# Attention in a decoder layer: the context products of two units issued together, behind the second score of every even unit

## The chip, the cores and the metric

One core of one Trainium2 chip. The metric is the device time of one execution of the whole program in microseconds; lower is better. The kernel before has a median of 1931.85 us over three runs (1931.19 to 1934.34).

## What is computed

A decoder layer on x of 8 sequences x 512 tokens x 512, in float32: a Mamba-2 block, a cross-attention and a soft mixture of experts, each added to its input and normalized. The change touches the cross-attention:

```python
q = (x @ Wq.T + bq).reshape(B, N, HEADS, HEAD_DIM).transpose(0, 2, 1, 3)
k = (context @ Wk.T + bk).reshape(B, M, HEADS, HEAD_DIM).transpose(0, 2, 1, 3)
v = (context @ Wv.T + bv).reshape(B, M, HEADS, HEAD_DIM).transpose(0, 2, 1, 3)
attn = jax.nn.softmax(jnp.einsum('bhnd,bhmd->bhnm', q, k) * scale, axis=-1)
out = jnp.einsum('bhnm,bhmd->bhnd', attn, v)
out = out.transpose(0, 2, 1, 3).reshape(B, N, C)
return out @ Wo.T + bo
```

B is 8, N = M = 512, 16 heads of 32 columns.

## The kernel before

The program runs three stages one after the other: `mamba_stage`, `attention_stage`, `moe_stage`. Inside a stage, each engine runs its own list of instructions, and semaphores tie them together. TensorE is called PE in the profile, ScalarE ACT, VectorE DVE, GpSimd POOL, SyncE SP (it issues most of the DMAs).

The attention takes one sequence per turn. The 16 heads lie in four groups (`gr`) of four heads (`AG`), and the 512 context rows in four tiles (`u`), so a turn has 16 units n = 4 gr + u. In the names of steps below, the three numbers are group, tile and head. The scores are computed twice, since the softmax needs the maximum of each query's row before the exponentials of the transposed scores:

- "p1" (L2156, PE): scores of one head with the queries on the partitions, into one of five *shared* PSUM banks. DVE takes the extreme of each row (L2026, "the maximum"), and ACT takes the exp with the row's sum (L1963, "sum"), in place; after that the bank is free.
- "split" and "neg": the four heads' maxima of a group are split in two, transposed by PE (L2162), copied by ACT (L1970) and written by DMA into two more rows of the stacked queries.
- "st" (L2174, PE): the transposed scores of one head and one context tile, with the maxima taken off, into one of two *scores* banks. ACT takes the exp (L1956) into `probs`, a buffer with two places, one per unit, used in turn.
- "av" (L2185, PE): the context product of one unit. Its four heads are four matmuls of 32 columns each, next to each other in the array; each is recorded twice, so a unit has eight records. The four tiles of a group add up in the bank `o_bank`.
- "recip", "inv", "norm", "osplit": DVE inverts the sums, POOL spreads them (L1910), PE transposes them (L2192), DVE copies them out (L2042) and multiplies `o_bank` with them (L2046), then splits the result (L2051, L2054).
- "qk", "v" (L2128) and "out" (L2202): the projections of q, k and v for the next turns and the output projection, each in two halves of six matmuls, also in shared banks. A q or k projection is copied by ACT (L1948) and then read by DVE (L2013); v is copied by DVE (L2020); an output tile is read by DVE (L2068). The bank is free after DVE's part.
- "xt", "c": transposes and splits of the next input.

One list sets the order of all this, for all engines: `attention_order`. For each unit it goes through four heads. At each head it puts the maxima that are due (`MAXIMA`, 64 per turn, some 22 heads ahead of the scores), the score, the sums that are to be done by now (`totals(left)` leaves that many for later, by `LAGS`), and half a projection where `HALF_AT` says so. After the fourth head of unit n it puts the product of unit n - 1. An engine that has no part in a step skips it. Two waits tie the products to the rest. The exp of a unit's first head needs the product of two units before, since it overwrites its place in `probs`:

```python
if h == 0 and (n >= 2 or not t.first()):
    act.wait_ge(av_done, t.at(UNITS, n - 1))
```

and a score needs the exp of two scores before, for its bank:

```python
pe.wait_ge(exp_ready, t.at(AG * UNITS, AG * n + h + 1 - SCORE_BANKS))
```

`bank_plan` deals out the shared banks in the order of the steps, and `take` on PE waits for the last reader of the bank. So the place of a step in the list also decides whose reader it waits for. The lists are unrolled for the first turn, for three steady turns in a loop, and for the last turn and what remains of it (`parts_of`, `over_attention`).

## Time and profile before

| | us |
|---|---|
| median of the runs (lowest, highest) | 1931.85 (1931.19, 1934.34) |
| profiled execution: span from its first to its last instruction | 1924.5 |
| PE busy in the span | 1825.8 (95%) |
| DVE busy | 1433.6 (74%) |
| ACT busy | 1266.8 (66%) |
| POOL busy | 468.5 (24%) |

The profiled execution's own time is not given apart from its span; the median of the three runs is 7.35 us above the span. The context products run from 879.0 to 1646 us of the span, which is the attention's stretch. Seven turns (seven of the eight sequences) take 97.7 to 101.7 us each there, five of them 99.8; the last is shorter, since nothing is projected ahead in it. Times in a timeline are counted from the start of the span. A matmul record of 512 columns is about 0.40 us long, but the next one starts 0.23 us after it, since they are pipelined: the distance of two starts is what it costs. The same holds, less so, for ACT and DVE.

### The profile page before, as it was taken

The numbers are of one execution on the slowest core, as the hardware profiler recorded it, in microseconds if no ns is written. First come the engines' busy times: TensorE is split into PE (matmuls) and PEld (weight loads), VectorE is DVE, ScalarE is ACT, GpSimd is POOL, SyncE is SP. The second block draws the span as 40 slices with busy tenths as digits, with TensorE's granted clock in tenths as the row PEclk, the third lists the DMA queues.
The fourth block names the chain that finished last, engine by engine and source line by source line (L and its number), as shares of the span: only waits on it lengthen the run. The fifth ranks groups of instructions, "written<-read, shape, count | busy, mean of one in ns | idle before, by whom it ended". The sixth has DMA issues, their size and how long they took to land. (4 is left out here: it accounts for less than half of the span.)

```text
span 1924.5 us, 39071 instructions
## 1 busy us (share of the span) xinstructions
PE 1825.8 (95%) x12780; PEld 1308.2 (68%) x12780; DVE 1433.6 (74%) x2902; ACT 1266.8 (66%) x3128; POOL 468.5 (24%) x661
## 2 busy tenths in 40 slices
PE   7899999999999999778999999999999999899988
PEld 5677777777787878555666666666666664588853
DVE  7978888888888888646786767777776766666348
ACT  5646454555555555348988888888989888366614
POOL 1312121212121313331323232322222233100006
PEclk9999999999999999889999999999999999899999
DMA  7113131313131312333343333434343423821266
GB/s 236 53 49 103 46 105 46 106 45 107 40 111 38 114 35 94 137 102 97 89 111 111 111 111 100 122 89 116 87 123 90 129 67 102 259 95 50 75 209 257
DMA packets 120045, 200.61 MB, mean 104 GB/s; under 512 B 23088, under 2 KB 44592, under 8 KB 119600
## 3 DMA queue, kind: packets, MB, share of 16 engines
q1 hardware_dynamic: 110640, 179.20, 30.1%
q0 software_dynamic: 9216, 18.89, 4.0%
q8 instruction: 118, 1.93, 0.4%
q14 instruction: 71, 0.58, 0.1%
HBM read 117.27 MB, written 29.88 MB: 76 GB/s over the span
## 5 line engine op out<-in xcount | busy, mean ns | idle before, releaser
L2026 DVE TENSOR_REDUCE a_mx<-a_shared 128x1 f32<-128x512 f32 x512 | 329.5, 681 | 56.6 <-PE a_shared L2156 54.5
L1963 ACT ACTIVATE a_shared<-a_shared,a_mx 128x512 f32<-128x512 f32 x512 | 340.9, 668 | 22.7 <-DVE a_mx L2026 22.2
L1956 ACT ACTIVATE a_probs<-a_scores 128x512 f32<-128x512 f32 x512 | 300.5, 600 | 67.9 <-PE a_scores L2174 64.7
L2156 PE MATMUL a_shared<-a_ks,a_qs 96*128 96x512 f32 x512 | 208.2, 427 | 14.5 <-ACT a_shared L1963 10.4
L2174 PE MATMUL a_scores<-a_qs,a_ks 98*128 98x512 f32 x512 | 201.2, 404 | 5.6 <-ACT a_probs L1956 5.5
L2128 PE MATMUL a_shared<-link 128*128 128x512 f32 x768 | 199.1, 395 | 1.1 <-DVE a_qk_lo L2013 1.1
L1083 PE MATMUL m_proj<-m_xt_hi,link 128*128 128x512 f32 x448 | 182.4, 407 | 3.8 <-DVE m_acc L777 3.4
L597 ACT ACTIVATE m_xw<-m_added,m_wdt 128x64 f32<-128x64 f32 x256 | 56.0, 329 | 192.5 <-DVE m_xdt L865 192.5
L2156 PEld LDWEIGHTS a_shared<-a_ks,a_qs 96*128 96x128 f32 x512 | 94.1, 190 | 129.2 <-ACT a_shared L1963 57.6
L1084 PE MATMUL m_proj<-m_xt_lo,link 128*128 128x512 f32 x448 | 177.1, 395 | 0.0
L1085 PE MATMUL m_proj<-m_xt_hi,link 128*128 128x512 f32 x448 | 176.2, 393 | 0.0
L777 DVE SCALAR_TENSOR_TENSOR m_acc<-m_proj,m_cw,m_acc 128x511 f32<-128x511 f32 (+2 forms) x216 | 159.3, 747 | 17.6 <-ACT m_acc L536 12.4
L2128 PEld LDWEIGHTS a_shared<-link 128*128 128x128 f32 x768 | 144.6, 190 | 34.7 <-DVE a_qk_lo L2013 1.5
L2185 PE MATMUL a_o_bank<-a_probs,a_v 128*32 128x512 f32 x1024 | 137.7, 610 | 0.0
L491 POOL TENSOR_TENSOR m_ssum<-m_ssum,m_sq 128x512 f32<-128x512 f32 x56 | 72.4, 1293 | 262.3 <-ACT m_sq L607 167.3
L2174 PEld LDWEIGHTS a_scores<-a_qs,a_ks 98*128 98x128 f32 x512 | 97.3, 191 | 34.1 <-ACT a_probs L1956 16.3
L1790 POOL DMA_DIRECT2D a_ks<-a_k_hi x192 | 95.2, 503 | 80.3 <-DVE a_qk_lo L2013 42.1
L1963 ACT ACTIVATION_READ_ACCUMULATOR a_shared<-a_shared,a_mx 128x1 f32 x512 | 109.5, 214 | 0.0
L1083 PEld LDWEIGHTS m_proj<-m_xt_hi,link 128*128 128x128 f32 x448 | 84.7, 189 | 27.8 <-DVE m_acc L777 7.5
L1085 PEld LDWEIGHTS m_proj<-m_xt_hi,link 128*128 128x128 f32 x448 | 84.5, 189 | 20.1
L1084 PEld LDWEIGHTS m_proj<-m_xt_lo,link 128*128 128x128 f32 x448 | 84.6, 189 | 16.7
L880 DVE SCALAR_TENSOR_TENSOR m_st<-m_st,m_whole,m_added 128x64 f32<-128x64 f32 x384 | 90.8, 278 | 6.8
(306 smaller groups left out, 3925.3 us busy)
## 6 DMA issues: line engine op xcount, KB each, us to landing
m_dec<-step_decay SPq DMA_DIRECT2D x64, 256.0 KB, 4.0
a_qs<-link SPq DMA_DIRECT2D x256, 64.0 KB, 2.0
m_ce<-run_decay SPq DMA_DIRECT2D x128, 112.0 KB, 3.1
a_ks<-a_k_hi POOLq DMA_DIRECT2D x192, 64.0 KB, 2.5
e_x<-x SPq DMA_DIRECT2D x11, 1024.0 KB, 5.6
m_xt_in<-x_t_in SPq DMA_DIRECT2D x8, 1024.0 KB, 9.2
m_x_tok<-x_in SPq DMA_DIRECT2D x8, 1024.0 KB, 5.3
x<-m_x_tok SPq DMA_DIRECT2D x32, 256.0 KB, 2.7
```

The lines of the kernel that those rows point to most:

```text
L777: ins = dve.scalar_tensor_tensor(out=acc[:, slot, s:SEQ], in0=proj[tile % 2][:, 0:SEQ - s], scalar=cw[:, n, 2 - i:3 - i], in1=acc[:, slot, ...
L1083: pe.matmul(bank[:, :], wh, xt_hi[:, k, :], start=(k == 0), stop=False)
L1084: pe.matmul(bank[:, :], wh, xt_lo[:, k, :], start=False, stop=False)
L1085: ins = pe.matmul(bank[:, :], wl, xt_hi[:, k, :], start=False, stop=(k == KT - 1))
L1790: eng.dma_start(dst[:, h, :].bitcast(F32), part[h * AD:(h + 1) * AD, :].bitcast(F32)).then_inc(stack_in[queue][gr % 2], 16)
L1956: act.activation(probs[:, n % 2, h, :], scores[t.score_bank(n, h)][:, :], ACT.Exp, scale=-1.0).then_inc(exp_ready, 1)
L1963: act.activation(scored[:, :], scored[:, :], ACT.Exp, scale=-1.0, bias=mx[:, i % 2, j, h:h + 1], accum_out=den[:, i, j, h:h + 1]).then_inc ...
L2026: dve.tensor_reduce(mx[:, i % 2, j, h:h + 1], bank(what)[:, :], AX.X, ALU.min).then_inc(mx_ready, 1)
L2128: ins = pe.matmul(bank(what)[:, :], *pair, start=(k == n == 0), stop=(k == KT - 1 and n == 2))
L2156: pe.matmul(bank(what)[:, :], qs[0:STACK, t.slot(i), h, j * P:(j + 1) * P], ks[0:STACK, t.slot(i), h, :], start=True, stop=True).then_inc( ...
L2174: pe.matmul(scores[t.score_bank(n, h)][:, :], ks[0:STACK + 2, t.slot(i), h, j * P:(j + 1) * P], qs[0:STACK + 2, t.slot(i), h, :], start=Tr ...
L2185: ins = pe.matmul(o_bank[rows, :], v[:, j, i * P + hh * AD:i * P + (hh + 1) * AD], probs[:, n % 2, hh, :], start=(j == 0), stop=(j == TT - 1))
```

## The change

The product of each unit no longer follows the next unit's fourth score. In an even unit, right behind its second score (`PAIR_AT = 1`), two products are issued in a row: in a group's first unit (u = 0) those of the last two tiles of the group before, after the transposes of the inverse sums and followed by the normalization; in its third unit (u = 2) those of the first two tiles of this group. Before the first score of an even unit all pending sums are put (`totals(0)`), and after the second unit of a group up to two may be left.

```diff
-LAGS = (2, 1, 0, 0)
+LAGS = (2, 1, 2)
+PAIR_AT = 1
...
+        group, d = (gr - 1, 0) if n >= TT else (KT - 1, -1)
         for h in range(AG):
             for _ in range(-(-(h + 1) * MAXIMA[n] // AG) - -(-h * MAXIMA[n] // AG)):
                 maximum()
                 totals(LAGS[0])
+            if h == 0 and u % 2 == 0:
+                totals(0)
             put("st", gr, u, h, 0)
-            totals(LAGS[1] if h < AG - 1 else LAGS[2])
+            totals(LAGS[1] if h < AG - 1 else LAGS[2] * (n % TT == 1))
             ended()
+            if h == PAIR_AT and u == 0:
+                put("inv", group, 0, 0, d)
+                for j in (TT - 2, TT - 1):
+                    put("av", group, j, 0, d)
+                put("norm", group, 0, 0, d)
+            elif h == PAIR_AT and u == 2:
+                for j in (0, 1):
+                    put("av", gr, j, 0, 0)
             for half in range(2):
                 if HALF_AT[n][half] == h:
                     large(n, half)
         if u == TT - 1:
             put("recip", gr, 0, 0, 0)
-        group, d = (gr - 1, 0) if n >= TT else (KT - 1, -1)
-        if u == 0:
-            put("inv", group, 0, 0, d)
-        put("av", *((gr, u - 1, 0, 0) if u else (group, TT - 1, 0, d)))
-        totals(LAGS[3])
-        if u == 0:
-            put("norm", group, 0, 0, d)
```

Five lines are added above the attention's code, so L2185 of the kernel before is L2190 after, and so on.

On PE, the end of unit 11 and unit 12 of a steady turn before. The rows are: p1 and the last score of unit 11, the product of unit 10, p1 and the first score of unit 12, half a k projection, and so on:

```order
L2156 MATMUL a_shared2<-a_ks,a_qs 128x512
L2174 MATMUL a_scores1<-a_qs,a_ks 128x512
L2185 MATMUL a_o_bank<-a_probs,a_v 32x512 x4
L2117 REGISTER_ALU
L2156 MATMUL a_shared3<-a_ks,a_qs 128x512
L2174 MATMUL a_scores0<-a_qs,a_ks 128x512
L2128 MATMUL a_shared4<-link 128x512 x6
L2117 REGISTER_ALU
L2156 MATMUL a_shared0<-a_ks,a_qs 128x512
L2174 MATMUL a_scores1<-a_qs,a_ks 128x512
L2128 MATMUL a_shared4<-link 128x512 x6
```

The same place after the change:

```order
L2161 MATMUL a_shared2<-a_ks,a_qs 128x512
L2179 MATMUL a_scores1<-a_qs,a_ks 128x512
L2122 REGISTER_ALU
L2161 MATMUL a_shared3<-a_ks,a_qs 128x512
L2179 MATMUL a_scores0<-a_qs,a_ks 128x512
L2133 MATMUL a_shared4<-link 128x512 x6
L2122 REGISTER_ALU
L2161 MATMUL a_shared0<-a_ks,a_qs 128x512
L2179 MATMUL a_scores1<-a_qs,a_ks 128x512
L2197 MATMUL a_shared1<-a_ident,a_inv_rows 128x128 x4
L2190 MATMUL a_o_bank<-a_probs,a_v 32x512 x8
L2133 MATMUL a_shared4<-link 128x512 x6
```

The product of unit 10 has left its place ahead of unit 12, and comes with that of unit 11 behind the transposes, between the two halves of the k projection. The first half of that projection writes shared4 in both, the bank that the q projection just before it used.

On ACT, the change from unit 11 to unit 12 before: two sums, the exps of unit 12's first two heads, a sum, and the copy of the k projection:

```order
L1963 ACTIVATE a_shared0,a_den<-a_shared0,a_mx 128x512
L1959 REGISTER_ALU
L1963 ACTIVATE a_shared2,a_den<-a_shared2,a_mx 128x512
L1955 REGISTER_ALU
L1956 ACTIVATE a_probs<-a_scores0 128x512
L1956 ACTIVATE a_probs<-a_scores1 128x512
L1959 REGISTER_ALU
L1963 ACTIVATE a_shared3,a_den<-a_shared3,a_mx 128x512
L1768 REGISTER_ALU
L1948 ACTIVATE a_k_hi<-a_shared4,bcol 128x512
```

And after:

```order
L1968 ACTIVATE a_shared0,a_den<-a_shared0,a_mx 128x512
L1964 REGISTER_ALU
L1968 ACTIVATE a_shared2,a_den<-a_shared2,a_mx 128x512
L1964 REGISTER_ALU
L1968 ACTIVATE a_shared3,a_den<-a_shared3,a_mx 128x512
L1960 REGISTER_ALU
L1961 ACTIVATE a_probs<-a_scores0 128x512
L1961 ACTIVATE a_probs<-a_scores1 128x512
L1773 REGISTER_ALU
L1953 ACTIVATE a_k_hi<-a_shared4,bcol 128x512
```

The third sum has moved ahead of the two exps, and nothing stands between them and the copy of the projection.

## Rows read from the trace of the kernel before

**Rows 1.** Windows of one steady turn: busy time (and instructions) of each engine, granted clock, DMA.
```profile
core 0: us, PE busy (x) PEld busy (x) DVE busy (x) ACT busy (x) POOL busy (x), PEclk, DMA share, GB/s
1045.90:1145.70 99.80, 99.03 (x499) 66.38 (x496) 73.85 (x137) 87.98 (x213) 27.86 (x46) 1.00 0.38 107
```

**Rows 2.** Timeline of PE, units 11 and 12: start us, us, instruction.
```profile
1137.70 0.40 PE L2128 MATMUL a_shared<-a_xt_hi,link 128*128 128x512 f32 x1
...
1139.08 0.39 PE L2156 MATMUL a_shared<-a_ks,a_qs 96*128 96x512 f32 x1
1139.31 0.39 PE L2174 MATMUL a_scores<-a_qs,a_ks 98*128 98x512 f32 x1
1139.63 1.07 PE L2185 MATMUL a_o_bank<-a_probs,a_v 128*32 128x512 f32 x8
1140.63 0.50 PE L2156 MATMUL a_shared<-a_ks,a_qs 96*128 96x512 f32 x1
1140.96 0.40 PE L2174 MATMUL a_scores<-a_qs,a_ks 98*128 98x512 f32 x1
1141.20 1.53 PE L2128 MATMUL a_shared<-link 128*128 128x512 f32 x6
1142.57 0.39 PE L2156 MATMUL a_shared<-a_ks,a_qs 96*128 96x512 f32 x1
```

**Rows 3.** Timeline of PE, windows 1113.40:1113.74 and 1113.40:1113.76: records begun.
```profile
1113.30 0.64 PE L2185 MATMUL a_o_bank<-a_probs,a_v 128*32 128x512 f32 x4
...
1113.30 1.04 PE L2185 MATMUL a_o_bank<-a_probs,a_v 128*32 128x512 f32 x5
```

**Rows 4.** Timeline of ACT, units 11 and 12; in brackets the idle time before.
```profile
1139.36 0.69 ACT L1948 ACTIVATE link<-a_shared,bcol 128x512 fp32r<-128x512 f32 x1
...
1143.23 0.60 ACT L1956 ACTIVATE a_probs<-a_scores 128x512 f32<-128x512 f32 x1 [0.50 <-PE a_scores L2174]
1143.73 0.66 ACT L1963 ACTIVATE a_shared<-a_shared,a_mx 128x512 f32<-128x512 f32 x1
...
1144.69 0.69 ACT L1948 ACTIVATE a_k_hi<-a_shared,bcol 128x512 fp32r<-128x512 f32 x1 [0.19 <-PE a_shared L2128]
1145.28 0.59 ACT L1956 ACTIVATE a_probs<-a_scores 128x512 f32<-128x512 f32 x1
1145.76 0.66 ACT L1963 ACTIVATE a_shared<-a_shared,a_mx 128x512 f32<-128x512 f32 x1
```

**Rows 5.** Timeline of DVE, units 11 and 12.
```profile
1140.08 0.75 DVE L2013 SCALAR_TENSOR_TENSOR a_qk_lo<-a_shared,bcol,link 128x512 fp32r<-128x512 f32 x1 [1.73 <-ACT link L1948]
```

**Rows 6.** Waits in 1000:1500 (total us, times, longest), then lines of DVE there.
```profile
ACT a_probs L1956 <- PE a_scores L2174: 38.4, 70, 1.2
...
L2020 DVE COPY a_v<-a_shared 128x512 f32<-128x512 f32 x20 | 13.8, 692 | 16.9 <-PE a_shared L2128 16.7
...
L2068 DVE TENSOR_TENSOR a_x_tok<-a_shared,a_x_tok 128x512 f32<-128x512 f32 x20 | 13.8, 691 | 6.5 <-PE a_shared L2202 6.5
```

**Rows 7.** Timelines of PE and of ACT in unit 8.
```profile
1119.26 0.40 PE L2156 MATMUL a_shared<-a_ks,a_qs 96*128 96x512 f32 x1
1120.18 0.50 PE L2156 MATMUL a_shared<-a_ks,a_qs 96*128 96x512 f32 x1 [0.52 <-ACT a_shared L1963]
...
1121.15 0.63 PE L2192 MATMUL a_shared<-a_ident,a_inv_rows 128*128 128x128 f32 x4 [0.25 <-POOL a_inv_rows L1910]
...
1119.36 0.65 ACT L1963 ACTIVATE a_shared<-a_shared,a_mx 128x512 f32<-128x512 f32 x1
1119.92 0.20 ACT L1963 ACTIVATION_READ_ACCUMULATOR a_shared<-a_shared,a_mx 128x1 f32 x1
1120.02 0.60 ACT L1956 ACTIVATE a_probs<-a_scores 128x512 f32<-128x512 f32 x1
```

**Rows 8.** Timeline of PE in the last turn.
```profile
1634.68 1.06 PE L2185 MATMUL a_o_bank<-a_probs,a_v 128*32 128x512 f32 x8
...
1636.87 0.99 PE L2174 MATMUL a_scores<-a_qs,a_ks 98*128 98x512 f32 x2 [0.45 <-ACT a_probs L1956]
...
1640.89 0.64 PE L2185 MATMUL a_o_bank<-a_probs,a_v 128*32 128x512 f32 x4
```

## The prediction

> **What bounds the kernel now.** I first read the windows of one steady turn of the attention (one sequence, 16 units). It takes 99.80 us, and PE is busy for 99.03 of them at a granted clock of 1.00; ScalarE (ACT) is busy for 87.98 and VectorE (DVE) for 73.85 [rows 1]. PE is the bound, with 0.77 us of idle time per turn. The change touches the attention alone, so everything else costs nothing here.
>
> Next the timeline of PE, to see what a visit to the 32-column products costs [rows 2]. A score before anything else starts 0.24 us ahead of the next matmul (1140.96 to 1141.20); before the products it is 0.32 (1139.31 to 1139.63). The eight product records take 1.00 us (1139.63 to 1140.63). The second four start between 0.44 and 0.46 after the first four (there are four records by 1113.74 and five by 1113.76 [rows 3]); I take 0.445 as the stream of each four. The rest, 1.00 - 0.89 = 0.11, passes before the next matmul starts, and that first full-width one needs 0.33 (1140.63 to 1140.96) instead of 0.23. One visit thus costs 0.08 + 0.11 + 0.10 = 0.29 us besides its streams.
>
> Then ACT and DVE beside it [rows 4, 5], since ACT's order is changed too. ACT has gaps, and they follow a pattern: it waits for an instruction that PE issues behind half a projection (the exp at 1143.23, 0.50 us; the copy of a k projection at 1144.69, 0.19 us). In 500 us it waits 38.4 us for scores [rows 6]. Today these gaps cost PE nothing, except at one place per turn: in unit 8 PE waits 0.52 us for a sum, to get a shared bank back [rows 7].
>
> **What is removed.** 16 visits per turn become 8. Saved: 8 x 0.29 = 2.3 us; I take 2.2, since some visits now follow other neighbours (transposes). Over the seven turns that are full of other work this is 15.4 us. The products themselves stay. No DMA and nothing in SP's or POOL's queue changes its place, and the inverse sums are asked for two scores later than before, so the 0.25 us that PE waited for them at the end of unit 8 [rows 7] goes too; it is inside the 0.77.
>
> The Trainium skill, TensorEngine Tiling (Array Packing), Tiling Modes, says that a change of tiling mode drains TensorE. By that rule, the trace agrees: it is the 0.29 us of each visit, and taken alone the rule would give the time of the first rival below.
>
> **What is added: ACT waits.** The exp of an even unit's first score overwrites the exponentials of two units before, so it waits for their product. Before, that product stood ahead of the score on PE. Now it stands behind the second score, so ACT is held at the head of its queue until the first product of the pair is done, and the sums that it had in reserve have been finished ahead. After the two exps that are then ready, its next work stands on PE behind the second product (0.96) and mostly half a projection (1.38; 1141.20 to 1142.57 [rows 2]). That is 1.4 to 2 us without work, in seven of eight pairs. ACT has 11.8 us per turn in all [rows 1], so it becomes late, and being late matters: scores need the exp of two scores before, and maxima need a shared bank, which a sum or DVE gives back.
>
> I walked a turn with these durations: a small matmul 0.235, half a projection 1.38; an exp holds ACT 0.48 (1145.28 to 1145.76) and PE may go on 0.66 after its start (0.60, and the 0.06 between the end of a sum, 1120.12, and PE's start at 1120.18 [rows 7]); a sum 0.66 (1119.36 to 1120.02); from the start of a projection's second half to its copy 1.66 (1137.70 to 1139.36), to the end of DVE's part 3.13 (to 1140.83) [rows 2, 4, 5]. From the end of the first product of unit 10 to that of unit 12, with t = 0 at the first of these two ends:
> - second product to 0.96, half of the k projection to 2.44, then two maxima and two scores, the turn of the maxima to 3.75. ACT: two exps to 1.15, idle to 2.7, the copy to 3.3; DVE is done at 4.17. PE's next maximum wants that bank: **0.48 idle**.
> - ACT, late by now, gives back what PE asks for at 5.1, 5.64, 7.4 and 9.56, where PE had arrived 0.17, 0.30, 0.14 and 0.07 before: **0.68 idle**.
> - the k projection of block 2 wants the bank of the q projection. Its second half starts at 7.64, so the bank is free at 10.77 at best, 10.97 with ACT late. PE gets there at 10.03: **0.93 idle**. Before, 0.37 us were to spare here (1140.83 against 1141.20), only because a product of 1.18 us, its switches included (0.08 + 1.00 + 0.10), stood between the two.
>
> Together 2.1 us. The other seven windows, in the same way: unit 0: 0.9 (banks of v that the removed products used to cover); unit 2: 0.3; unit 4: 0.1; unit 6: 0.4; unit 8: 1.8 (two halves of q stand behind the pair, ACT idles over 2 us, a maximum waits 1.0 for a sum, a score 0.8 for an exp); unit 12: 1.5 and unit 14: 1.5. Sum 8.6 us per turn.
>
> How good is such a walk? I did the same for unit 8 of the kernel before and got 0.77 us of idle time where the trace has 0.52 [rows 7], and none around units 12 and 13, as in the trace. So it finds the places and overstates by up to a third. The waits are between 5.8 (two thirds) and 8.6 us. They replace the 0.77. Net per turn: 5.8 - 0.8 - 2.2 = +2.8 to 8.6 - 0.8 - 2.2 = +5.6; I take the middle, **+4.2**, as neither end has a better claim.
>
> The Trainium skill, TensorE: Matmul & The Clock Gate, on the array's architectural detail, says that ScalarE's queue is strictly first in, first out. By that rule, the trace agrees: the sum at 1143.73 runs only behind the exp that waited until 1143.23 [rows 4]. A queue that let ready sums pass would hide most of the new gaps and make the first rival the likelier one.
>
> **The small edits.** DVE's copy of the inverse sums is now followed by a normalization that waits for two products: it is held about 0.8 us more, four times per turn. DVE has 26 us of room and the next maximum stands behind half a projection on PE; nothing, or up to 0.2 us each time if a maximum is already there (5.6 us in all, kept for the upper end). In the last turn there is little but scores and products; a pair of units takes 6.2 us there (1634.68 to 1640.89) with waits of 0.45 for exps [rows 8], and my walk of the new order gives 6.1: nothing.
>
> **Sum.** 7 x 4.2 = +29 us. The profiled execution's span is 1924.5, so its new span would be about 1954; the median of the runs, 7.35 us above that span, goes from 1931.85 to **1961 us**.
>
> **Rivals.**
> 1. *PE stays the bound; faster.* ACT's 11.8 us of room absorb all new gaps, and only the 2.2 us per turn are seen: 1931.85 - 15.4 = 1916. For it: PE waited nowhere but in unit 8 although ACT waits often [rows 6, 7]. Against it: the bank of the q projection in unit 12, where 0.37 us of room meets 1.18 us of cover taken away, whatever ACT does. It decides as long as PE's waits stay under 3.0 us per turn (2.2 + 0.8). Chance 0.13.
> 2. *Only the banks bite.* ACT is never late; three places are left where a product covered a bank. Unit 12 costs 1.18 - 0.37 = 0.8. Before the second maximum of unit 2 and of unit 4, a bank is wanted 1.38 + 2 x 0.235 = 1.85 us after a second half starts, and free after 1.54 (the half's records), DVE's 0.69 [rows 6] and 0.06, so 0.44 later; twice. Unit 8 keeps its 0.5. That is 2.2 us of waits, 2.2 - 0.8 - 2.2 = -0.8 per turn, 1926. This lies about on the border between faster and no change. Chance 0.12.
> 3. *The pair saves nothing.* The second product's weights load as slowly as after a full-width matmul, so the 2.2 us stay, and the waits come on top: +6.4 per turn, 1976. Against it: within a visit the second four start without a gap. Chance 0.07.
> 4. The forecast: slower, 1945 to 1978. Chance 0.68.
>
> What a measurement of this kernel can tell from no change is 0.2%, 3.9 us. Slower: 0.68 + 0.07 = 0.75. Rival 2 is split evenly: faster 0.13 + 0.06 = 0.19, same 0.06. The range reaches down to 1922, so that it takes in rival 2 and leaves out most of rival 1, and up to 1980: the walk undiscounted (1971) with DVE's part (5.6) and a little more. Within the forecast's own case the range is 1945 to 1978.
>
> **What would show it.** In the changed profile: product groups of 16 records lasting about 1.9 us, with the second unit's four records 0.45 after the first's last four (right for the gain). A turn of 102.5 to 105.5 us with PE busy about 97 of it. PE waits for ACT in units 8, 10, 12 and 14; before the k projection of unit 12 a gap near 0.9 that DVE's copy ends. ACT waiting over 1 us after two exps in a row, for a score or a projection. I would be wrong if a turn is under 99.6 us: then ACT was late without PE noticing, and the walk's bank and exp waits would be missing from PE's list.

## The result, and the profile after

The changed kernel takes **2075.5 us** (median; 2065.24 to 2081.86), the kernel before 1932.1 beside it: a ratio of 1.074, 95% interval 1.072 to 1.076. That is 143 us slower. The forecast was 1961, with a range up to 1980: the sign was right, and the size a fifth of what came.

The page of the changed kernel, profiled in an execution of 2078.28 us: its span, then the busy time of each engine.

```profile
span 2076.5 us, 39071 instructions
PE 1886.3 (91%) x12780; PEld 1316.3 (63%) x12780; DVE 1437.1 (69%) x2902; ACT 1266.3 (61%) x3128; POOL 465.0 (22%) x661
```

ACT and DVE do the same work as before (1266.8 and 1433.6 us). PE is busy for 60 us more, though it has no more to do. Some of its time is slow work: matmuls at half the clock, and matmuls behind a short wait, which last 0.50 us in the rows instead of 0.40. The window of one steady turn answers to [rows 1] (the same columns), 99.80 us then and 119.00 now:

```profile
1050.60:1169.60 119.00, 105.73 (x500) 66.56 (x499) 74.18 (x136) 87.55 (x212) 26.99 (x45) 0.96 0.32 90
```

PE is idle for 13.3 us of it (0.77 before) and busy for 6.7 us more, at a granted clock of 0.96 (1.00 before). The longest waits in that window (us in total, times, longest):

```profile
ACT a_probs L1961 <- PE a_o_bank L2190: 10.5, 5, 6.7
...
ACT a_probs L1961 <- PE a_scores L2179: 8.3, 8, 2.4
PE a_shared L2197 <- POOL a_inv_rows L1915: 7.6, 3, 5.2
ACT a_shared L1968 <- DVE a_mx L2031: 6.2, 8, 1.8
```

The first line, the forecast's own mechanism, looks like the cause. PE's largest wait, however, is for the inverse sums that POOL spreads: 7.6 us. The timeline of PE in unit 8 shows 5.19 of them at one place, where [rows 7] have 0.25:

```profile
1162.65 0.50 PE L2161 MATMUL a_shared<-a_ks,a_qs 96*128 96x512 f32 x1 [0.94 <-ACT a_shared L1968]
1162.98 0.39 PE L2179 MATMUL a_scores<-a_qs,a_ks 98*128 98x512 f32 x1
1168.57 1.09 PE L2197 MATMUL a_shared<-a_ident,a_inv_rows 128*128 128x128 f32 x4 [5.19 <-POOL a_inv_rows L1915]
1169.58 3.43 PE L2190 MATMUL a_o_bank<-a_probs,a_v 128*32 128x512 f32 x16
```

What POOL does meanwhile, and DVE's reciprocal, the first link of that chain:

```profile
1162.77 3.00 POOL L1795 DMA_DIRECT2D a_ks<-a_k_hi  x6 [5.04 <-DVE a_qk_lo L2018]
1166.33 1.48 POOL L1795 DMA_DIRECT2D a_ks<-a_qk_lo  x3 [0.55 <-issue]
1167.80 0.62 POOL L1915 COPY a_inv_rows<-a_inv 128x512 f32<-128x512 f32 x1
```
```profile
1162.14 0.24 DVE L2044 RECIPROCAL a_inv<-a_den 128x16 f32<-128x16 f32 x1
```

The same on POOL and DVE in the kernel before:

```profile
1115.36 3.00 POOL L1790 DMA_DIRECT2D a_ks<-a_k_hi  x6 [6.05 <-PE a_scores L2174]
1118.92 1.47 POOL L1790 DMA_DIRECT2D a_ks<-a_qk_lo  x3 [0.55 <-issue]
1120.38 0.62 POOL L1910 COPY a_inv_rows<-a_inv 128x512 f32<-128x512 f32 x1
```
```profile
1114.73 0.24 DVE L2039 RECIPROCAL a_inv<-a_den 128x16 f32<-128x16 f32 x1
```

The inverse sums were ready at 1162.38, but the copy that spreads them stands in POOL's queue behind nine DMA issues of a stacked key, 5 us from the first issue to the copy. Before, that was so too, and it did not matter: PE asked at the end of unit 8, 0.25 us too soon. The change asks behind the second score, two scores and a projection **earlier**. The reciprocals of the other groups have no stack ahead of them, but come late as well: 0.76 us in unit 0 and 1.65 in unit 4.

The clock follows the idle time. Windows of 2 us around that wait:

```profile
1162.00:1164.00 2.00, 0.73 (x2) 0.30 (x2) 2.00 (x6) 1.21 (x4) 1.23 (x3) 1.00 0.24 55
1164.00:1166.00 2.00, 0.00 (x0) 0.00 (x0) 1.14 (x2) 0.83 (x4) 1.77 (x4) 0.96 0.71 187
1166.00:1168.00 2.00, 0.00 (x0) 0.00 (x0) 0.00 (x0) 0.00 (x0) 1.68 (x4) 0.50 0.42 92
1168.00:1170.00 2.00, 1.44 (x8) 0.92 (x12) 0.31 (x1) 0.00 (x0) 0.42 (x1) 0.50 0.29 64
1170.00:1172.00 2.00, 2.00 (x12) 0.40 (x8) 0.38 (x1) 0.42 (x1) 0.00 (x0) 0.50 0.00 0
1172.00:1174.00 2.00, 2.00 (x13) 0.88 (x6) 0.69 (x1) 1.34 (x4) 0.00 (x0) 0.83 0.00 0
```

PE stands still from 1163.4, the granted clock falls from 2.4 to 1.2 GHz (0.50) just before 1166, and it comes back after 1172. In that time PE issues the transposes and the pair: 16 product records take 3.43 us instead of 1.92. A second, shorter fall comes in unit 0. Some 7.6 us of work per turn run at half speed, which costs 3.8 us.

The pair itself is as forecast:

```profile
1066.90 0.39 PE L2179 MATMUL a_scores<-a_qs,a_ks 98*128 98x512 f32 x1
1067.22 1.92 PE L2190 MATMUL a_o_bank<-a_probs,a_v 128*32 128x512 f32 x16
1069.07 1.19 PE L2133 MATMUL a_shared<-link 128*128 128x512 f32 x4
```

Its 16 records take 1.85 us to the next start, against 4 x 0.445 = 1.78 of streams. Two visits before cost 2 x 0.29 = 0.58 besides the streams, one pair 0.08 + 0.07 + 0.10 = 0.25.

To see where the rest went, I laid the distances between the first scores of successive units beside each other. These numbers are worked out from the timelines of PE (median of four steady turns, us; the last two lines are runs of the next section):

```
unit                 0     1     2     3     4     5     6     7     8     9    10    11    12    13    14    15   turn
before             6.49  5.85  6.06  5.87  6.30  6.47  6.91  5.35  8.18  5.83  6.27  5.83  6.25  5.84  6.27  6.06   99.8
after              9.97  5.53  7.35  5.60  9.03  5.33  8.12  4.29 17.24  5.69  7.76  5.39  9.01  4.89  7.29  5.83  118.3
recip early        8.24  5.53  7.32  5.67  7.68  5.32  8.13  4.29 10.01  5.70  7.75  5.38  8.99  4.88  7.30  5.80  108.0
unpaired, moved    7.23  5.87  6.71  5.88  6.91  6.63  6.97  5.37  9.15  6.45  6.93  5.99  8.22  6.06  6.44  6.56  107.4
```

An even unit now holds the products of two units, so even and odd are read together. Units 8 and 9 lose 8.9 us; the other seven pairs lose 0.2 to 3.2 each. (The turn in the table is the sum of the medians. Counted from the first score of a turn to that of the next, the changed kernel's seven turns take 117.2, 117.4, 119.3, 121.9, 117.3, 119.2 and 119.3 us, with a median of 119.2; those of the kernel before take 98.3 to 100.9, with a median of 99.8.)

### The profile page after: what moved, and what is told of

It is laid out like the page before. It is cut to its first block and busy times, and to the rows that moved or that the text cites. A ratio compares the mean times of both kernels' runs of the same rounds, so it can differ in the third digit from the quotient of the medians.

```text
span 2076.5 us, 39071 instructions
## 1 busy us (share of the span) xinstructions
PE 1886.3 (91%) x12780; PEld 1316.3 (63%) x12780; DVE 1437.1 (69%) x2902; ACT 1266.3 (61%) x3128; POOL 465.0 (22%) x661
## 5 line engine op out<-in xcount | busy, mean ns | idle before, releaser
L1961 ACT ACTIVATE a_probs<-a_scores 128x512 f32<-128x512 f32 x512 | 294.9, 600 | 150.3 <-PE a_o_bank L2190 83.5
L2179 PE MATMUL a_scores<-a_qs,a_ks 98*128 98x512 f32 x512 | 209.2, 421 | 12.0 <-ACT a_probs L1961 9.4
L2133 PE MATMUL a_shared<-link 128*128 128x512 f32 x768 | 205.5, 403 | 7.8 <-DVE a_qk_lo L2018 5.4
L2133 PEld LDWEIGHTS a_shared<-link 128*128 128x128 f32 x768 | 139.8, 189 | 76.6 <-issue 27.3
L2190 PE MATMUL a_o_bank<-a_probs,a_v 128*32 128x512 f32 x1024 | 150.3, 714 | 0.0
L1915 POOL COPY a_inv_rows<-a_inv 128x512 f32<-128x512 f32 x32 | 19.7, 616 | 392.8 <-DVE a_inv L2044 392.8
L2133 PE MATMUL a_shared<-a_xt_hi,link 128*128 128x512 f32 x256 | 95.2, 419 | 4.8 <-ACT a_shared L1968 2.7
L1085 PEld LDWEIGHTS m_proj<-m_xt_hi,link 128*128 128x128 f32 x448 | 84.4, 188 | 20.2
```

The source lines that it names most:

```text
L1085: ins = pe.matmul(bank[:, :], wl, xt_hi[:, k, :], start=False, stop=(k == KT - 1))
L1961: act.activation(probs[:, n % 2, h, :], scores[t.score_bank(n, h)][:, :], ACT.Exp, scale=-1.0).then_inc(exp_ready, 1)
L2133: ins = pe.matmul(bank(what)[:, :], *pair, start=(k == n == 0), stop=(k == KT - 1 and n == 2))
L2179: pe.matmul(scores[t.score_bank(n, h)][:, :], ks[0:STACK + 2, t.slot(i), h, j * P:(j + 1) * P], qs[0:STACK + 2, t.slot(i), h, :], start=Tr ...
L2190: ins = pe.matmul(o_bank[rows, :], v[:, j, i * P + hh * AD:i * P + (hh + 1) * AD], probs[:, n % 2, hh, :], start=(j == 0), stop=(j == TT - 1))
```

## The experiments

Two theories stood at the start: **A**, the inverse sums are asked for too early (from the trace above); **B**, the forecast's own, ScalarE is held by the exponential buffer. Ratios are to the kernel before, run beside each experiment on the same chip; its medians lay between 1930.6 and 1933.2 us.

### The reciprocal one unit earlier in the changed kernel

```diff
-        if u == TT - 1:
-            put("recip", gr, 0, 0, 0)
...
         for half in range(2):
             if HALF_AT[n][half] == AG:
                 large(n, half)
...
+        if u == TT - 2:
+            put("recip", gr, 0, 0, 0)
```

> The changed kernel, but the inversion of a group's sums (DVE) and their spreading (POOL) are put at the end of the group's third unit, ahead of the stack's DMAs, instead of at the end of its fourth. Theory A (PE waits for the inverse sums, because they are asked for two scores earlier and in unit 8 POOL issues nine DMAs ahead of them; the clock falls with that idle time): the waits of 5.2, 1.7 and 0.8 us per turn and most of the 10 us at the lower clock (worth 3.8) go, a turn falls from 119.3 to about 108, the kernel from 2076 to about 1996. Theory B (ScalarE held by the exponential's buffer is the cause): a turn stays at 117 or more, 2060 or more.

Measured: **1996.7 us**, ratio 1.033 (1.031 to 1.036). This takes 78.8 of the 143 us away. The copy now runs ahead of the DMA issues, and the clock stays at 1.00:

```profile
1050.81 0.62 POOL L1915 COPY a_inv_rows<-a_inv 128x512 f32<-128x512 f32 x1 [19.04 <-DVE a_inv L2044]
1054.25 2.94 POOL L1795 DMA_DIRECT2D a_ks<-a_k_hi  x6 [2.83 <-PE a_scores L2179]
```
```profile
1060.00:1168.00 108.00, 102.14 (x498) 66.01 (x497) 73.71 (x137) 87.36 (x212) 27.09 (x46) 1.00 0.35 99
```

The turn fell by 11.2 us (119.2 to 108.0): 7.6 of waits and 3.8 of half clock are 11.4.

### The inverse sums earlier in the kernel before

```diff
...
+            if h == 1 and u == 0:
+                put("inv", group, 0, 0, d)
...
-        if u == 0:
-            put("inv", group, 0, 0, d)
```

> The kernel before, with one step moved: the transposes of the inverse sums stand behind the second score of a group's first unit, as in the change; every product stays where it was, unpaired. Theory A: PE waits about 5.3 us in unit 8, 1.9 in unit 4 and 0.6 in unit 0, and perhaps some us at the lower clock: 7.8 to 11 us per turn more, 1987 to 2010. Theory B: nothing, 1932.

Measured: **1997.4 us**, ratio 1.034 (1.032 to 1.036). The same wait, in a kernel in which nothing else is changed:

```profile
1029.32 1.09 PE L2192 MATMUL a_shared<-a_ident,a_inv_rows 128*128 128x128 f32 x4 [5.18 <-POOL a_inv_rows L1910]
```

One step moved by two scores and a projection costs 66 us. With the run before, theory A is shown from both sides.

### Three exponential buffers, with and without the early reciprocal

```diff
+PROBS = 3
...
-                        act.wait_ge(av_done, t.at(UNITS, n - 1))
-                    act.activation(probs[:, n % 2, h, :], scores[t.score_bank(n, h)][:, :], ACT.Exp,
+                        act.wait_ge(av_done, t.at(UNITS, n + 1 - PROBS))
+                    act.activation(probs_of(t, n)[:, h, :], scores[t.score_bank(n, h)][:, :], ACT.Exp,
```

The third buffer takes the room of the output weights' low part, in whose place the high part is added.

> The changed kernel with three places for the exponentials instead of two, so that ScalarE need not wait for a product before it overwrites one. (The low part of Wo is left out of the output projection to make the room; its matmuls are issued with the high part instead, so PE's work is the same.) Theory A: ScalarE's hold goes, but PE still stops at the inverse sums: 2040 to 2076, the waits of my walk that came from ScalarE (some 5 us per turn) at most are won. Theory B: a turn falls by 12 us or more, under 1990.

> Both edits: inverse sums early and three places for the exponentials (low part of Wo left out as before). Theory A with the pair's saving of 2.2 us per turn: only the bank waits are left (0.8, 0.4, 0.4), a turn is 98.5 to 101, the kernel 1920 to 1942. If the pair itself costs something that neither edit touches, it stays over 1960.

Measured: **2074.4 us** (1.072 to 1.076 times before) with the buffer alone, and **1997.6 us** (1.031 to 1.036) with both: each within 1.1 us of the time without the buffer. Theory B is wrong as a cause. So is the sum that stood for theory A in the second run (1920 to 1942): only its other branch, over 1960, came true. The waits of ACT in a steady turn with both edits, 1090 to 1198:

```profile
ACT a_shared L1976 <- DVE a_mx L2039: 6.0, 9, 1.4
ACT a_k_hi L1961 <- PE a_shared L2140: 5.9, 3, 3.1
ACT a_probs L1969 <- PE a_scores L2186: 5.4, 4, 2.3
...
ACT link L1961 <- PE a_shared L2140: 2.3, 1, 2.3
```

ACT no longer waits for a product, and waits as long for the next thing in its list (in all 20.8 us in this turn, and 20.2 in the turn with two buffers, of which 2.3 for products): a maximum, or the copy of a projection that PE issues behind the pair. A wait taken off an engine that then has nothing to do is no gain.

### The order of the sums

If the sums finished ahead are at fault (theory C), it must show alone in the kernel before, and must help when taken back. Against it stands theory D: the place of the products.

```diff
+            if h == 0 and u % 2 == 0:
+                totals(0)
             put("st", gr, u, h, 0)
-            totals(LAGS[1] if h < AG - 1 else LAGS[2])
+            totals(LAGS[1] if h < AG - 1 else 2 * (n % TT == 1))
...
-        totals(LAGS[3])
```

> The kernel before with only the sums' order of the change: all pending sums ahead of an even unit's first score, two left at the end of a group's second unit, none forced elsewhere. Products, inverse sums and reciprocal stay where they were. Theory C: 4 to 8 us more per turn, 1960 to 1990 us. Theory D: as before, 1929 to 1937 us.

Measured: **1971.5 us**, ratio 1.021 (1.018 to 1.024). PE's waits there, 1000 to 1400:

```profile
PE a_scores L2175 <- ACT a_probs L1957: 12.2, 12, 2.2
PE a_shared L2157 <- ACT a_shared L1964: 4.2, 5, 1.3
```

ACT takes a sum whose maximum is not there yet (it waits 23.9 us for maxima there, 8.6 in the kernel before), and the exps of ready scores stand behind it; PE, which waits 12.2 us for exps there, waited 0.5 in the kernel before. So the sums' order costs 39 us in the old order. The opposite run takes `totals(0)` out of the changed order (with the early reciprocal and three buffers; with two buffers the sums cannot lag, since the held exp would stand ahead of sums whose banks the product's predecessors on PE need, so there is no such run):

> The change with the reciprocal behind the third unit and three exponential buffers, as in the run that had both, and now the sums lag behind as before: the totals(0) ahead of an even unit's first score is left out. As there, the output projection adds the high part of its weights in place of the low, so the output differs; the instructions are as many. Theory C (the sums finished ahead make ScalarE wait for maxima that VectorE is just taking, and that wait is the remaining 8.2 us per turn): a turn of 100 to 103 us, 1935 to 1958 us, and ScalarE's waits for VectorE's maxima mostly gone. Theory D (the products no longer stand at the ends of the units, where they covered the shared banks): no change against that run, a turn near 108, 1990 to 2000 us.

Measured: **1996.4 us**, ratio 1.034 (1.031 to 1.036). Nothing comes back: theory C is wrong for this order. ACT's waits for maxima did fall, from 25.5 us in the run with both edits to 8.3, but those for scores rose from 22.5 to 34.1, and those for projections stayed (32.7 and 32.8). From 1000 to 1400:

```profile
ACT a_k_hi L1959 <- PE a_shared L2138: 21.8, 12, 2.7
...
ACT link L1959 <- PE a_shared L2138: 11.0, 4, 2.7
ACT a_shared L1974 <- DVE a_mx L2037: 8.3, 25, 0.6
```

The kernel before has 5.7 us in 13 such waits for projections.

### Pairs at the unit's end

The old order, with the pair behind the fourth score of even units, three buffers, the inverse sums in their old place:

> The kernel before with one thing of the change: two products in a row, but at the end of the even units (behind the fourth score), with the sums' lags as before; three exponential buffers, since the first of the pair comes one unit later than before (output projection as in the other run with three buffers), and the v projection of unit 14 swapped with the qk projection of unit 15. If pairing itself is worth the 2.2 us per turn of the prediction and the place does the harm (theory D): a turn near 98, 1914 to 1925 us. Theory C says the same, as no sum is finished ahead. If the pair itself is bad wherever it stands (two products in a row starve ScalarE for scores): a turn of 103 us or more, over 1950 us.

Measured: **1956.2 us**, ratio 1.012 (1.009 to 1.015). It is slower by 24 us, though the pairs save their 2.5 us per turn (by the starts at the products in its trace). That is the branch in which the pair is bad wherever it stands (over 1950; its turns take 102.2 to 104.3 us). It is also 40 us better than the run above (1996.4), with the pair behind the second score, so the place seems to matter; but the two runs differ in the inverse sums and in one swap of projections too.

### The early reciprocal alone in the kernel before

> The kernel before with only the reciprocal one unit earlier. Its inverse sums kept TensorE waiting 0.25 us once per turn; that may go: 1929 to 1932 us. This shows that the earlier reciprocal is by itself neither a gain nor a loss, so that what it gave back in the changed kernel was the wait for it.

Measured: **1925.8 us** (ten runs), ratio 0.997 (0.9955 to 0.9988). It is 0.3% faster than the kernel before, by 6.8 us, a little more than expected. Unit 8 goes from 8.18 to 7.75 us, seven times: 3 us of it; the rest was not traced. So of the 78.8 us that the same edit gave back in the changed kernel, some 7 were to be had anyway. This is the base that the next runs are read against.

### Single products at the place of the change, and at other places

Theory E: what costs is 3.3 us (two products, half a projection) in which PE gives ACT nothing. Then single products at the same place should be harmless, and the pair's place without a projection behind it better.

```diff
...
             ended()
+            if h == 1:
+                if u == 0:
+                    put("inv", group, 0, 0, d)
+                put("av", *((gr, u - 1, 0, 0) if u else (group, TT - 1, 0, d)))
+                if u == 0:
+                    put("norm", group, 0, 0, d)
...
```

The same steps at the unit's end are taken out, and the reciprocal is early.

> The kernel before with the reciprocal one unit earlier and every product, one by one, moved from behind the fourth score of a unit to behind the second score of the same unit (inverse sums and normalization with it); sums' lags as before, two exponential buffers, which hold nothing, since the product of unit n - 1 still stands ahead of the scores of unit n + 1. Theory E (what costs is two products in a row, mostly with half a projection behind them: 3.3 us in which TensorE gives ScalarE nothing to do): about as with the early reciprocal alone, 1924 to 1940 us. Theory D (the place at the unit's end covered the shared banks): near 1990 us.

```diff
-HALF_AT = [(1, 2), (1, 3), (1, 3), (1, 3), (1, 3), (0, 2), (0, 2), (1, 2), (1, 1), (0, 1),
-           (0, 1), (1, 2), (0, 1), (0, 1), (0, 1), (1, 2)]
+HALF_AT = [(2, 3), (1, 3), (2, 3), (1, 3), (2, 3), (0, 2), (2, 3), (1, 2), (2, 3), (0, 1),
+           (0, 3), (1, 2), (0, 3), (0, 1), (0, 3), (1, 2)]
```

> The changed order with the reciprocal early, three exponential buffers (output projection as in the other runs with three buffers) and the sums lagging as before, and now the halves of projections that stood right behind the pair (seven even units) moved one or two scores later. Theory E: TensorE gives ScalarE work 1.4 us sooner after each pair; at least half of the remaining 8.2 us per turn goes, a turn of 101 to 104 us, 1940 to 1965 us. Theory D, or the deal of the banks: a turn of 107 us or more, over 1985 us.

Measured: single products **1979.3 us**, ratio 1.026 (1.024 to 1.028), 53 us over the early reciprocal alone; the halves moved off the pair **2034.0 us**, ratio 1.054 (1.052 to 1.057), worse by 38. Theory E fails in both, although half of the 38 us is the clock: PE stops for up to 2.7 us in units 10 and 12 there, the granted clock from 1000 to 1400 is 0.97 (1.00 in the run with which it is compared), and half of PE's time at 0.50 comes to 3.4 us per turn, an estimate. In the first of these the turn is 107.4 us without any pair, hold or sum ahead, and the loss sits mostly in the even units, in 8 and 12 above all, as in the changed kernel (table above). PE's longest gaps in one turn of it are 0.93 and 0.76 in unit 8, for sums, and these two in unit 12,

```profile
1157.72 1.65 PE L2129 MATMUL a_shared<-link 128*128 128x512 f32 x6 [0.71 <-DVE a_qk_lo L2014]
1164.49 0.50 PE L2157 MATMUL a_shared<-a_ks,a_qs 96*128 96x512 f32 x1 [0.70 <-DVE a_qk_lo L2014]
```

for banks that VectorE's copy of a projection gives back late. The next three runs ask whether a simple rule makes the place bad: behind the half of a projection instead of ahead of it, for single products and for the pair, and behind the third score.

> As the run with unpaired products behind the second score, but where half a projection stands behind that score too, the product now comes behind the half instead of ahead of it. Theory D (a product is the cover under which the reader of a projection's bank, ScalarE or VectorE, finishes, and moved ahead of the half it covers nothing): at least half of the loss of 49 us goes, 1930 to 1955 us, and the waits for VectorE's copies of q and k in units 9 to 14 are gone. Theory F (the tables MAXIMA and HALF_AT are matched to products at the units' ends as regards ScalarE's supply, and any other place starves it): no better than 1965 us.

> Unpaired products behind the third score (and behind a half that stands there) instead of the second. Theory D: where the second half of a projection stands behind the second score (six units of sixteen) the product now follows two scores later, as before it followed four instructions later, so most of those banks are covered: 1930 to 1955 us. Theory F: a loss that grows with the distance from the old place, so between 1926 and 1979, near 1950 us: this run alone does not tell them apart, the one beside it does.

> The changed order with the reciprocal early, three exponential buffers (output projection as in the other runs with three buffers) and sums lagging as before, with the pair now behind the half projection of the same score instead of ahead of it. Theory D: from 1996 down to 1945 to 1975 us, a turn of 101 to 105 us. Theory F: stays at 1985 to 2000 us.

Measured: **1993.8 us** (1.029 to 1.035 times before), **1964.8 us** (1.014 to 1.019) and **1998.9 us** (1.032 to 1.037). Theory D, in the form that a product must follow a half, is wrong: single products do worse behind it, and the pair no better. All three times lie where theory F put them, but theory F names no place that should be good, and no run changes its tables. The distances of these runs show why no simple rule holds: in the first, behind the half, unit 8 is back at 8.19 us from 9.15, but units 9, 11, 13 and 15 have become 7.15, 6.77, 6.55 and 7.01 (5.81, 5.83, 5.84 and 6.06 in the base). A likely reading, not shown bank by bank: wherever the 1.08 us of a product are put, some banks gain cover that did not need it and others lose cover that did.

### Late banks or a late ScalarE?

Two edits, in the changed kernel with the early reciprocal, and both in the base as a control:

```diff
-                    dve.scalar_tensor_tensor(out=qk_lo[:, j, i % 2, :], in0=bank(what)[:, :],
+                    dve.scalar_tensor_tensor(out=qk_lo[:, j, i % 2, :], in0=qk_hi[j][:, i % 2, :].bitcast(F32),
...
-                    "qk": (qk_split[j % 2], KT, i + 1),
+                    "qk": (qk_hi_s[j % 2], KT, i + 1),
```
```diff
-                    act.activation(scored[:, :], scored[:, :], ACT.Exp, scale=-1.0, bias=mx[:, i % 2, j, h:h + 1],
+                    act.activation(scored[:, 0:SEQ // 2], scored[:, 0:SEQ // 2], ACT.Exp, scale=-1.0, bias=mx[:, i % 2, j, h:h + 1],
```

> The changed kernel with the reciprocal early (1997 us, a turn of 108.0), and now VectorE's low parts of q and k are computed from the high part in SBUF in place of the PSUM bank, so that the bank is free after ScalarE's copy, about 1.5 us sooner (the low parts come out wrong; as many instructions). Theory D' (late banks): the 1.8 us per turn that TensorE waits for VectorE's copies go, with what each wait brings on besides: 3 to 5 us per turn, 1960 to 1978 us. Theory G (ScalarE is late, and holds everything else): under 1.5 us per turn, 1986 us or more.

> The changed kernel with the reciprocal early, and ScalarE's sums over 256 of the 512 columns (the other half of each sum is left out), which makes ScalarE some 17 us per turn lighter. Theory G (ScalarE is late after it was starved behind the pair, and has too little room to catch up): most of the 8.2 us per turn goes, a turn of 99 to 102 us, 1925 to 1950 us. Theory D' (banks of projections, late whatever ScalarE does): the waits for VectorE's copies stay, 1970 us or more.

> Both edits of the two runs before in the changed kernel with the reciprocal early. If late banks and a late ScalarE are the whole of the remaining loss, PE alone is left as the bound, and the pairs show their gain: a turn of 96.5 to 98 us, 1905 to 1918 us. If the loss is in TensorE itself (the pair's place among the transposes, say): still over 1950 us.

> The control: both edits in the kernel before with the reciprocal early. It is bound by TensorE with 0.3 us of idle time per turn, so nothing is to be had: 1920 to 1928 us. Its distance to the run with both edits in the changed order is what the pairs are worth by themselves: 12 to 18 us by the prediction's 2.2 us per turn.

Measured: bank early **2006.1 us** (1.035 to 1.041 times before), short sums **1969.7** (1.018 to 1.022), both **1977.0** (1.020 to 1.024), control **1941.9** (1.003 to 1.006). The short sums fall between the two theories, and the control misses its 1920 to 1928. The other two lie in the second branch of their expectations, but these times cannot be taken for it, since the edit of the bank has a fault of its own: it made things slower, in the control too, where unit 13 takes 9.75 us instead of 5.84. DVE there, and POOL beside it:

```profile
1044.45 4.45 DVE L2013 SCALAR_TENSOR_TENSOR a_qk_lo<-a_k_hi,bcol 128x512 fp32r<-128x512 f32 x1 [1.73 <-ACT a_k_hi L1948]
```
```profile
1043.74 4.60 POOL L1900 TENSOR_TENSOR a_x_tok<-a_x_tok,a_brow 128x2048 f32<-128x2048 f32 x1
```

An operation of 0.75 us takes 4.45 beside one of POOL. The last run cuts POOL's to 32 columns:

```diff
-                    pool.tensor_tensor(x_tok[:, :, :], x_tok[:, :, :],
-                                       brow[:, :].unsqueeze(1).to_broadcast([P, TT, DM]), ALU.add)
+                    pool.tensor_tensor(x_tok[:, :, 0:8], x_tok[:, :, 0:8],
+                                       brow[:, 0:8].unsqueeze(1).to_broadcast([P, TT, 8]), ALU.add)
```

> The control with both edits, and GpSimd's addition of the output bias cut from 2048 to 32 columns (the rest of the bias is left out). In the control one VectorE operation per turn, the low part of k, takes 4.45 us instead of 0.75, beside GpSimd's addition of 4.60 us, since the edit had given it SBUF operands alone. If the addition is what holds it: the operation takes 0.5 to 0.8 us everywhere, unit 13 goes back from 9.75 to 5.84 us, the turn to 99.2, and the time from 1942 to 1912 to 1920 us. If it is something else in that place (a wait on data): unchanged, 1940 us or more.

Measured: **1918.5 us**, ratio 0.993 (0.991 to 0.994), as expected if the addition is what holds it, and unit 13 is back at 5.84:

```profile
1040.92 0.27 POOL L1900 TENSOR_TENSOR a_x_tok<-a_x_tok,a_brow 128x32 f32<-128x32 f32 x1
```
```profile
1041.62 0.75 DVE L2013 SCALAR_TENSOR_TENSOR a_qk_lo<-a_k_hi,bcol 128x512 fp32r<-128x512 f32 x1 [1.73 <-ACT a_k_hi L1948]
```

So the runs with the bank given back early carry a fault of their own: unit 13 is 3.9 us longer in the control, and 2.3 and 1.9 in the changed order, where the operation takes 2.9 us. Their times say nothing on banks. Their units say a little: in unit 12 of the changed order, where PE waits longest for VectorE's copy, the edit takes 1.4 us off (8.99 to 7.57, and 9.08 to 7.66 with short sums); units 10 and 11 together take 13.05 us with it and 13.13 without. What all banks are worth stays open, since GpSimd's addition was cut in the control alone. What can be read is the short sums: a turn of 104.8 us instead of 108.0, so they take away 3.2 of the 8.2 us per turn, and 27 us of the time, of which the last turn has 8.4. In the control, short sums with the rest take 0.3 off a turn of 99.4 and 7.3 us off the time, so some 20 us are left for a late ACT. The other 5 us per turn stay although ACT is busy for only 286.80 of 400 us (short sums, 1000 to 1400):

```profile
1000.00:1400.00 400.00, 381.96 (x1877) 253.39 (x1875) 278.60 (x513) 286.80 (x802) 106.79 (x173) 1.00 0.37 103
```

## Why the prediction was wrong

The step that failed first is the third below. It is not the only one: with its cost taken away (1996.7 us) the change is still 36 us above the forecast, and 17 above the upper end of its range. By its own steps:

- **PE is the bound, ACT and DVE have room.** Right; in the control, where nothing is late, a turn takes 99.1 us against 99.8.
- **The pair saves 2.2 us per turn.** Right. A pair has 0.25 us of switches where two visits had 0.58, eight times: 2.6; over a whole turn with the early reciprocal, the starts at the products sum to 2.2 less than before. The Trainium skill, TensorEngine Tiling (Array Packing), Tiling Modes, has a change of mode drain TensorE; by that rule, the trace agrees: half the changes, and a bit over half the cost is gone. Rival 3 falls.
- **"The inverse sums are asked for two scores later than before."** This is the step that failed, and it is a plain misreading: they moved from behind the fourth score of the group's first unit to behind its second, two scores earlier. I looked for where the products went and took the sums along with them. The sentence before it, that nothing in POOL's queue changes its place, is true and was no comfort: the one who waits for POOL had moved. [Rows 7] held the warning, since a wait of 0.25 us there means no slack at all. To ask for something some 5 us sooner that was already 0.25 us late costs 5 us. Price: 7.6 us of waits per turn and 3.8 us of half clock, which the sum did not consider; 78.8 us in all, shown by two runs.
- **ACT held by the exponential buffer.** The wait is there (10.5 us in the turn of the changed kernel, most of it a consequence of the inverse sums), and it costs nothing: with a third buffer the time is the same, with and without the early reciprocal. The mechanism named for the 29 us was wrong. What the walk called "held, then without work" was "without work" in either case, because sums finished ahead, projections and scores all stand on PE behind the pair.
- **The walk of the waits, 5.8 to 8.6 us per turn.** The discount mixed two measures. The walk counts by how much a matmul starts late. Measured so, with the inverse sums out of the way, the starts behind full-width matmuls that are over 0.13 us late sum to 8.9 us per turn (18 of them), where the kernel before has 1.1 (2); the undiscounted walk said 8.6. The 0.52 in unit 8 and the 0.77 of the turn are the profile's idle time, which is shorter: the matmul that waited 0.52 us in [rows 7] starts 0.92 after the one before it instead of 0.235, so 0.69 late, and the walk's 0.77 for it was not a third too much. Measured as idle time, the 8.9 are 5.9 (108.00 - 102.14). The agreement of 8.6 with 8.9 is in part luck: for the windows from unit 0 on, in order, the walk has 0.9, 0.3, 0.1, 0.4, 1.8, 2.1, 1.5 and 1.5, and the trace 0.7, 0.7, 0.6, 1.1, 1.9, 1.2, 1.1 and 1.5; and the hold that the walk rests on costs nothing.
- **The bank of the q projection in unit 12, 0.93 us.** Right in place and releaser: a gap of 0.62 ahead of the k projection, ended by DVE's copy. Three more of this kind follow the pairs of units 10 (0.19, where the walk had 0.48), 12 (0.70) and 14 (0.53, in the next turn's first unit). The gap in unit 12, and the one of 0.70:

```profile
1079.04 1.65 PE L2133 MATMUL a_shared<-link 128*128 128x512 f32 x6 [0.62 <-DVE a_qk_lo L2018]
...
1086.71 0.50 PE L2161 MATMUL a_shared<-a_ks,a_qs 96*128 96x512 f32 x1 [0.70 <-DVE a_qk_lo L2018]
```

- **A gap costs itself.** Wrong. Besides the long gaps, 40 starts per turn are 0.05 to 0.13 us late with the early reciprocal, against 27 before. At the products there are 12 fewer, as forecast; elsewhere there are 25 more, which cost 2.5 us per turn. 15 of them are the next start after a long gap: the matmul that ended the gap lasts 0.50 us in the rows instead of 0.40, and the one behind it starts 0.10 late.
- **The last turn: nothing.** Wrong, and the clock is most of it. Its 64 scores take 93.7 us instead of 77.0, and 89.6 with the early reciprocal. In its first half the waits are those of the other turns (0.85 and 1.77 us for inverse sums). In its last eight units, where the walk had 6.1 us for a pair of units against 6.2, units 12 and 13 take 8.1 us against 6.6. The last turn before, changed, and changed with the early reciprocal; the granted clock stands behind POOL's time:

```profile
1566.52:1643.56 77.04, 71.39 (x336) 39.53 (x334) 52.92 (x106) 63.41 (x151) 24.39 (x29) 0.98 0.38 117
```
```profile
1702.03:1795.70 93.67, 82.19 (x344) 42.39 (x343) 57.02 (x110) 65.19 (x155) 24.39 (x29) 0.87 0.38 113
```
```profile
1623.39:1712.99 89.60, 80.42 (x344) 42.36 (x343) 56.56 (x109) 64.79 (x155) 23.74 (x28) 0.88 0.39 119
```

  Half of PE's time at 0.50 comes to 10.6 us with the early reciprocal and 1.7 before, an estimate: 9 of the 12.6 us that this turn costs without the inverse sums. Its stops are short there (none over 1.12 us), but PE is busy for only 90% of the turn.

Sum of a turn, from 99.8: long gaps +7.8, short ones +1.3 (after what the pairs save there is taken off), the rest of the pairs' saving inside the visits -0.9: +8.2, as measured. Then the inverse sums 7.6 and the clock 3.8: +19.6, where the steady turns went from 99.8 to 119.2.

Of the 143 us, **79 are settled** (inverse sums behind POOL's DMA issues, and the clock that falls with them). Of the other **65**, some 9 are the clock of the last turn. It is shown that the place of the products is enough for most (53 us for single products over the base), that the order of the sums alone costs 39 and the pair at the old place 24, that such parts overlap instead of adding up (the changed order with the early reciprocal is 71 us over the base, less than the three together), and that a lighter ACT takes 27 away, some 20 of them more than in the old order. It is not settled how the rest divides between banks and chains of PE, DVE and ACT: each single wait of ACT that was taken away handed its time to the next. That the tables of maxima, halves and lags fit the old place of the products, and no other that was tried, describes all these runs; as a cause it is only argued.

## What to carry to other kernels

When a step is moved, compare its place before and after in the full order with everything that it waits for, and read the wait it had before: one that ends with 0.25 us of waiting has no slack, and every microsecond sooner is paid in full, and more if PE's clock falls meanwhile. In a schedule that is full on one engine, first find the one step that is asked for too early (here worth 79 us, and 7 us even in the kernel before) before reordering the bulk. An in-order engine that is starved gained nothing here from one wait less: take away one wait and look whether its total idle time fell, or only changed its name.

## What was not expected of the hardware

- After 2.5 us without a matmul (1163.4 to just before 1166) the granted clock went from 1.00 to 0.50, the 1.2 GHz level, and the matmuls that followed ran at it until after 1172. It fell after a shorter stop too. In the control, PE stood still for 2.10 us up to 1050.15 (the matmuls of 1050 to 1054 at half the clock):

```profile
1050.15 0.50 PE L2156 MATMUL a_shared<-a_ks,a_qs 96*128 96x512 f32 x1 [2.10 <-ACT a_shared L1963]
```
```profile
1048.00:1050.00 2.00, 0.05 (x1) 0.00 (x0) 2.00 (x3) 0.46 (x2) 0.34 (x1) 1.00 0.29 72
1050.00:1052.00 2.00, 1.85 (x5) 1.50 (x6) 1.88 (x4) 1.64 (x5) 0.00 (x0) 0.66 0.00 0
1052.00:1054.00 2.00, 2.00 (x6) 1.55 (x5) 0.71 (x2) 0.97 (x3) 0.00 (x0) 0.50 0.00 0
```

  The Trainium skill, TensorE: Matmul & The Clock Gate, Part 1, has the clock fall to 1.2 GHz when TensorE is idle; by that rule, the trace agrees. In the last turn with the early reciprocal (above) the clock fell although no stop was over 1.12 us. A sum of waits must therefore ask what runs behind them, and not behind the long ones alone.
- A DVE operation of 512 columns whose two tensors are both in SBUF took 4.45 us beside a POOL addition of 4.60 us that had begun 0.71 us before it, and 0.75 without it. With one tensor in PSUM the same line takes 0.75 beside the same addition, begun 0.72 us before it (DVE, then POOL, in the base):

```profile
1048.76 0.75 DVE L2013 SCALAR_TENSOR_TENSOR a_qk_lo<-a_shared,bcol,a_k_hi 128x512 fp32r<-128x512 f32 x1 [1.73 <-ACT a_k_hi L1948]
```
```profile
1048.04 4.60 POOL L1900 TENSOR_TENSOR a_x_tok<-a_x_tok,a_brow 128x2048 f32<-128x2048 f32 x1
```

  The Trainium skill, SBUF — State Buffer, Who interferes with whom, says that a DVE instruction with two SBUF inputs contends with a GpSimd one that reads SBUF, and that one with at most one SBUF input, outside the modes with two ports, does not; by that rule, the trace agrees, and my edit had walked into it. A bank given back sooner was paid for with this.
